# Two-layer graph kernel on one NeuronCore: half of the late node products from two-part operands, edge sums begun eleven tiles earlier, 29 gathers ahead of the stores

## What is computed

```python
edge_index = jnp.stack([src, dst])
x = _layernorm(x + gnn0(x, edge_index, node_vec, ...))     # all nodes
x = _layernorm(x + gnn1(x, edge_index, edge_weight, ...))  # edges, then per destination

# gnn0
neighbor_sum = segment_sum(x[col], row)                    # gather by edge, sum by node
mean_neighbor = neighbor_sum / max(deg, 1)
h_mean = (x + mean_neighbor) * 0.5 @ W_mean + b_mean
h_concat = concat([x @ W_ego + b_ego, mean_neighbor @ W_nb + b_nb])
gate = sigmoid(gate_weight * node_vec + gate_bias)
out = (1 - gate) * h_mean + gate * h_concat
```

## Time and profile before

| | |
|---|---|
| median of 3 runs | 2863.28 us |
| the profiled execution | 2864.34 us |
| its span, first to last instruction | 2862.5 us |
| busy in the span: PE, DVE, ACT, POOL | 92%, 84%, 65%, 55% |
| TensorE's granted clock, mean | 0.973 |
| float32 node products, line 961 | 1564 matmuls, 495 ns each as modelled |
| DMA traffic | 653.5 MB |

### The profile page before, as it was taken

How to read it: one execution, slowest core, us unless ns; L and a number is a source line. 1 busy time by engine, 2 the same in 40 slices (tenths; PEclk the granted TensorE clock), 3 DMA queues, 4 the chain that set the end, 5 groups by cost and what they waited for, 6 DMA issues and landing times. The chain is left out here.

```text
span 2862.5 us, 53163 instructions
## 1 busy us (share of the span) xinstructions
PE 2641.2 (92%) x14009; PEld 1610.8 (56%) x14009; DVE 2393.4 (84%) x7769; ACT 1851.0 (65%) x3839; POOL 1582.5 (55%) x1491
## 2 busy tenths in 40 slices
PE   4699989999999499999999999999999999976774
PEld 2466668788887255555555555555555555543442
DVE  8888877777777688888888888888888888878996
ACT  2355555666665277777777777777777777757885
POOL 0476727777776555454545454545455555306776
PEclk9799999999999699999999999999999999989998
DMA  9899986666665587777777777777777777647894
GB/s 346 298 350 350 351 295 202 198 199 203 203 204 183 155 211 220 213 220 214 220 213 222 214 222 212 219 218 221 213 223 213 222 212 217 180 131 239 276 281 149
DMA packets 544668, 653.52 MB, mean 228 GB/s; under 512 B 244334, under 2 KB 451882, under 8 KB 544550
## 3 DMA queue, kind: packets, MB, share of 16 engines
q1 hardware_dynamic: 468518, 440.38, 52.2%
q0 software_dynamic: 69472, 208.99, 23.4%
q10 hardware_dynamic: 6560, 2.84, 0.4%
HBM read 315.65 MB, written 299.10 MB: 215 GB/s over the span
## 5 line engine op out<-in xcount | busy, mean ns | idle before, releaser
L1242 ACT ACTIVATE hidT<-bank,b1c 128x512 f32<-128x512 f32 x490 | 336.7, 687 | 414.3 <-PE bank L1532 340.4
L1151 POOL TENSOR_TENSOR u_hc<-u_hc 128x1536 f32<-128x1536 f32 x98 | 270.1, 2756 | 550.9 <-issue 429.4
L961 PE MATMUL bank<-w_node,xT 128*128 128x384 f32 x1564 | 558.6, 495 | 15.1 <-ACT bank L584 15.0
L1532 PE MATMUL bank<-xh,w1h 128*128 128x512 f16 x1568 | 469.2, 381 | 23.3 <-DMA xh<-eh 15.7
L1532 PE MATMUL bank<-xl,w1h 128*128 128x512 f16 x1568 | 468.2, 380 | 0.0
L1532 PE MATMUL bank<-xh,w1l 128*128 128x512 f16 x1568 | 468.2, 380 | 0.0
L584 ACT ACTIVATE bank<-bias_all 128x512 f32<-128x512 f32 x391 | 234.3, 599 | 235.7 <-DVE H L689 234.3
L961 PEld LDWEIGHTS bank<-w_node,xT 128*128 128x128 f32 x1564 | 288.5, 193 | 161.4 <-ACT bank L584 17.2
L1548 PE MATMUL bank<-hidT,w2f 128*64 128x256 f32 x3136 | 360.1, 382 | 0.8 <-ACT hidT L1242 0.8
L1373 DVE STREAM_TRANSPOSE feat<-catT 32x256 f32<-32x256 f32 x784 | 342.5, 437 | 17.0 <-ACT catT L1251 2.4
L1354 DVE TENSOR_SCALAR hidT<-bank,b1c 128x512 f32<-128x512 f32 x294 | 220.6, 750 | 120.7 <-PE bank L1532 112.3
(11 more groups left out here) (255 smaller groups left out, 5199.3 us busy)
## 6 DMA issues: line engine op xcount, KB each, us to landing
hc_tab<-H SPq DMA_DIRECT2D x78, 680.0 KB
er<-edge_tab SPq DMA_DIRECT2D x98, 512.0 KB, 4.4
X<-in_x SPq DMA_DIRECT2D x78, 640.0 KB, 5.2
h_row<-hc_tab SPq DMA_DIRECT2D x97, 512.0 KB
out_x<-o_row SPq DMA_DIRECT2D x97, 512.0 KB, 5.0
edge_tab<-u_x SPq DMA_DIRECT2D x98, 256.0 KB, 3.9
edge_tab<-feat SPq DMA_DIRECT2D x98, 256.0 KB
hc_tab<-zero_row SPq DMA_DIRECT2D x18, 1344.0 KB
```

The source lines that it names most:

```text
L961: ins = t_.matmul(p[:, 0:384], xT[t // 2 % XR][:, t % 2, c * P:(c + 1) * P], w_node[:, c, :], start=False, stop=c == 1, skip_group_check=True)
L1151: g.tensor_tensor(c, c, u_hc[s][:, :, MULT:MULT + 3].unsqueeze(3).to_broadcast([P, 4, 3, P]), ALU.mult).then_inc(u_scaled, 1)
L1242: a.activation(hidT[m][:, :], bank[2 + m % 2][:, :], ACT.Relu, bias=b1c[:, m:m + 1])\
L1532: ins = t_.matmul(bank[2 + m % 2][:, :], w[:, c, m * P:(m + 1) * P], xx[s][:, :, :].rearrange("p (k c) e -> p c k e", c=2)[:, c, :, :], st ...
```

## The change

It edits the node block and one piece of the setup:

- From pair `SPLIT` = 92 on, every other pair of node tiles (92, 94, ... 194: 52 pairs, 104 tiles) has its product made from split operands: ACT's copy goes to `xhigh` (short type F32R), DVE makes `xlow` = bank 0 minus `xhigh` (`low_x`), and PE makes six matmuls a tile (high by high weight, high by low weight, low by high weight, for two halves) instead of two float32 products.
- `low_x(p)` stands in DVE's `side` of step 2p-3, one step behind ACT's copy of that pair. The `turn` of pair p+1, on PE's step 2p-2, now waits for it, since it reads bank 0.
- The setup makes `w_nodeh` and `w_nodel` on DVE.
- `xT` has 3 buffers instead of 4.
- `PUT_LAG` 13 becomes 29; `DECODE` 16 becomes 20; `SUMS` 195 becomes 184 and `SPAN` 177 becomes 188, so that the edge sums begin eleven tiles earlier and end at the same tile.

```diff
+        w_nodeh, w_nodel = sb("w_nodeh", [P, 2, 384], F32R), sb("w_nodel", [P, 2, 384], F32R)
...
                 st.done(v.tensor_copy(w_nbh[:, :, :], w_nb[:, :, :]))
-                st.wait()
+                st.done(v.tensor_copy(w_nodeh[:, :, :], w_node[:, :, :]))
+                st.wait()
+                st.done(v.tensor_tensor(w_nodel[:, :, :], w_node[:, :, :], w_nodeh[:, :, :].bitcast(F32),
+                                        ALU.subtract))
...
-        XR = 4
+        XR = 3
...
+        XS = 2
+        xlow = [tmp(f"xlow{b}", [P, 2, D], F32R) for b in range(XS)]
+        xhigh = [tmp(f"xhigh{b}", [P, 2, D], F32R) for b in range(XS)]
...
-        PUT_LAG = 13
+        PUT_LAG = 29
-        SORT, PHASES, DECODE, SUMS, SPAN, FIX = 0, 7, 16, 195, 177, 377
+        SORT, PHASES, DECODE, SUMS, SPAN, FIX = 0, 7, 20, 184, 188, 377
+        SPLIT = SUMS // 2 // 2 * 2
+        SPLITS = tuple(range(SPLIT, NT // 2 + 1, 2))
...
+                    to = xhigh[nth(p) % XS] if in_parts(p) else xT[p % XR]
...
+                def low_x(p):
+                    many = min(2, NT + 1 - 2 * p)
+                    dve.wait_ge(xt_copied, p + 1)
+                    if nth(p) >= XS:
+                        dve.wait_ge(p_ready, 2 * SPLITS[nth(p) - XS] + 2)
+                    q = nth(p) % XS
+                    v.tensor_tensor(xlow[q][:, 0:many, :],
+                                    bank[0][:, 0:many * D].rearrange("p (t d) -> p t d", t=many),
+                                    xhigh[q][:, 0:many, :].bitcast(F32), ALU.subtract).then_inc(x_low, 1)
...
+                    if now % 2 == 1 and in_parts((now - 1 + LEAD_X) // 2):
+                        low_x((now - 1 + LEAD_X) // 2)
...
                 def turn(p):
-                    if p:
+                    if in_parts(p - 1):
+                        pe.wait_ge(x_low, nth(p - 1) + 1)
+                    elif p:
                         pe.wait_ge(xt_copied, p)
...
+                    if in_parts(pair):
+                        pe.wait_ge(x_low, nth(pair) + 1)
...
+                            for part_, w in ((high, w_nodeh), (high, w_nodel), (low, w_nodeh)):
+                                n += 1
+                                ins = t_.matmul(p[:, 0:384], part_[:, c * P:(c + 1) * P], w[:, c, :], start=False,
+                                                stop=n == 6, skip_group_check=True)
```

More of the change, by code:

```diff
@@ L383, in build @@
         H = [tmp(f"H{r}", [P, HALF, HU]) for r in range(HR)]
-        XR = 4
+        XR = 3
         xT = [tmp(f"xT{b}", [P, 2, D]) for b in range(XR)]
+        XS = 2
+        xlow = [tmp(f"xlow{b}", [P, 2, D], F32R) for b in range(XS)]
+        xhigh = [tmp(f"xhigh{b}", [P, 2, D], F32R) for b in range(XS)]
+        x_low = sem("x_low")
         stats = tmp("stats", [P, TEN, 6])
@@ L444, in build, with nth, in_parts @@
         LASTR = (ET - 1) % AC
-        PUT_LAG = 13
-        SORT, PHASES, DECODE, SUMS, SPAN, FIX = 0, 7, 16, 195, 177, 377
+        PUT_LAG = 29
+        SORT, PHASES, DECODE, SUMS, SPAN, FIX = 0, 7, 20, 184, 188, 377
+        SPLIT = SUMS // 2 // 2 * 2
+        SPLITS = tuple(range(SPLIT, NT // 2 + 1, 2))
+        def nth(p):
+            return (p - SPLIT) // 2
+        def in_parts(p):
+            return p in SPLITS
         PRODS = (5, 6, 7)
@@ L575, in copy_x @@
                     many = min(2, NT + 1 - 2 * p)
-                    a.activation(xT[p % XR][:, 0:many, :], bank[0][:, 0:many * D].rearrange("p (t d) -> p t d", t=many),
+                    to = xhigh[nth(p) % XS] if in_parts(p) else xT[p % XR]
+                    a.activation(to[:, 0:many, :], bank[0][:, 0:many * D].rearrange("p (t d) -> p t d", t=many),
                                  ACT.Copy).then_inc(xt_copied, 1)
@@ L958, in product @@
                     p = bank[NODE[t % 3]]
-                    pe.wait_ge(xt_copied, t // 2 + 1)
+                    pair = t // 2
+                    if in_parts(pair):
+                        pe.wait_ge(x_low, nth(pair) + 1)
+                        high, low = xhigh[nth(pair) % XS][:, t % 2, :], xlow[nth(pair) % XS][:, t % 2, :]
+                        n = 0
+                        for c in range(2):
+                            for part_, w in ((high, w_nodeh), (high, w_nodel), (low, w_nodeh)):
+                                n += 1
+                                ins = t_.matmul(p[:, 0:384], part_[:, c * P:(c + 1) * P], w[:, c, :], start=False,
+                                                stop=n == 6, skip_group_check=True)
+                        ins.then_inc(p_ready, 1)
+                        return
+                    pe.wait_ge(xt_copied, pair + 1)
                     for c in range(2):
```

## The result

The changed kernel takes 3024.67 us (median of 3 runs, 3018.76 to 3028.46) against 2863.28: a ratio of 1.0557, 95% interval 1.0542 to 1.0572. That is 161 us slower, where 8.9 slower (2872.2) was forecast, and far outside the range of 2843 to 2880. The profiled execution spans 3022.9 us against 2862.5.

What follows compares the result with a forecast made beforehand. PE was taken as the bound from 444 to 924 us. Setup +1.4, keys and sums -0.5, split +8.0 gave +8.9 on 2864.34: 2873.2 us profiled, 2872.2 us median; range 2843 to 2880, for 8 in 10.

Steps and rivals of the forecast that it cites:

- Rest: `xT` with three buffers, the end of the sums and all later blocks: no effect, 0 us.
- Setup, +1.4: Setup block: two more DVE operations on 128x768 for the weight parts add 1.4 us, between 0 and 1.5.
- Keys: Node block, read of the keys: four tiles, 6.0 us, move into DVE's 7.28 us wait; node tiles gain 6.0.
- Start of the sums: Node block, tile 184: first sum waits for its gather until 373.8; DVE stands 6.7 us, eating the gain.
- Last fill and the new wait: Node block: first scatter at 435.0 after the last zero fill; PE stands 8.8 us at step 207, until 441.2.
- the term -0.5: Node block, later keys and earlier sums together: the wait of 8.34 changes its cause and stays; -0.5 us.
- Split, +8.0: Node block, 46 pairs from 104 on: 25 waits for `xlow` cost 28.2 us, savings 20.2, net +8.0.
- The three bare places: Earlier trace, `turn` with only one product before it: DVE's low part would come late, waits 0.95, 1.16, 1.48 us.
- The clock rule: Node block: frequent waits of about 1 us among PE's matmuls could make the clock swing; taken as 0.
- the fourth rival: Node block: the clock swings, each of 25 bare waits costing 2.8 us: +70, 2942 us; chance 0.03.
- Rivals 1 to 3: Node block: bank 0 free in time, 2844.0 us, 0.20; fills in before scatters, 2860.6, 0.14; scatters become the bound, 2879, 0.10.

Runs made afterwards that it cites:

- the run with eight fills: The changed kernel with eight one-column fills on DVE ahead of its edge loop: 2878.40 us, ratio 1.0051 to the kernel before.
- the longer loop: The kernel before, DVE's edge loop head 104 instructions into a 256-instruction block, 24 more instructions (semaphore steps) a round: 2949.85 us in one run.
- slot 104: The kernel before with DVE's edge loop head placed 104 instructions into a 256-instruction block, so the body crosses its end: 2864.74 us in one run.
- the announced jump: The changed kernel with `hint_back_edge=True` on DVE's edge loop instead of a placed head; the text gives no time.

## Why the prediction was wrong, step by step

- **The step that failed** is "*Rest*": "The end of the sums and all later blocks keep their place, 0." Their order on the engines did stay, and their place in the work too; what did not was the place of DVE's loop in its own instruction stream. The change adds 104 instructions ahead of it, and that cost 147 us. That the shift ended at a dear slot is chance: with eight instructions more, the same change is 146 us faster. No rival had it: all of them stand in the block that the change edits. What could be seen beforehand: a loop on DVE behind the edit, 104 instructions, an `instruction` queue in the list. What could not: the slot that the loop has on the chip, and that a shift would be dear.
- **The node block** came out at 13.6 us by PE's first edge row (11.8 in the run with eight fills), 8.9 were forecast: right in sign and kind.
- *Setup, +1.4.* DVE's last part of the weights ends at 29.29 against 28.06: +1.2.
- *Keys.* The wait of 7.28 is down to 0.86 (1.3 forecast), and the read stands at 108.33:

```profile
108.33 0.26 DVE L780 TENSOR_SCALAR ids_at<-raw 128x196 int32<-128x196 int32 x1 [0.86 <-DMA edge_raw<-srt_tab]
```

- *Start of the sums.* DVE's wait for the first gather is there, 7.84 in place of 6.7, and the first sum runs at 375.75, not 373.8 (before: the earlier trace rows):

```profile
375.75 1.08 DVE L901 SCALAR_TENSOR_TENSOR acc<-acc,same,xg 128x256 f32<-128x256 f32 x2 [7.84 <-DMA xg<-in_x,pay]
```

PE stood 9.82 behind it, until 379.22:

```profile
379.22 1.11 PE L984 MATMUL bank<-ident,X 128*128 128x128 f32 x4 [9.82 <-DVE xlow L872]
```

The prediction used the wait to eat the gain, and left out what comes after: the granted clock of 366 to 389 us is 0.78, where before it was 1.00.
- *Last fill and the new wait.* The fill went out at 429.25 (425.5 forecast), the first scatter at 438.94 (435.0), and PE's new wait is there, 9.99 (8.8):

```profile
438.94 1.04 POOL L559 DMA_INDIRECT hc_tab<-cn,idx_s  x1 [31.02 <-DMA hc_tab<-zero_row]
```

```profile
446.12 0.66 PE L1042 MATMUL bank<-w_nbh,accT 128*128 128x384 f32 x1 [9.99 <-ACT cn L631]
```

Two stands of about 10 us in place of one of 8.34, and the second ends at 446.12 where 441.2 was reckoned: the term -0.5 measured +3.8 without the split. Of these 4.9 us too late, 3.9 were there at the first scatter, in the sum up to the last fill. Inside the node block this is the term that was mis-sized.
- *Split, +8.0.* Waits on the `turn` line for `xlow`, 444 to 924 us (25, 28.2 us forecast):

```profile
PE bank L984 <- DVE xlow L872: 19.0, 22, 1.9
```

That is 0.86 a wait where 0.95 to 1.48 was taken. With the setup it was to cost 9.4, and alone it measured 8.8 by PE's rows and 12.0 by the runs (7.4 to 16.9). The three bare places in the earlier trace rows foretold the waits in kind, but that the sum was met is partly luck. In the run with eight fills PE waits 18.7 us for `xlow`, and the edge block begins 8.0 later than without the split, 1.2 of them the setup; so the pairs saved an estimated 18.7 - 6.8 = 12 us where 20.2 were reckoned. Waits and savings were both taken too large, by 8 to 10 us, and the errors cancelled.
- *The clock rule.* The granted clock of 444 to 924 us is 0.99, but what is missing lies right behind the stand that ends at 446.12: from 444 to 460 us it is 0.80, and from 460 to 924 us, where all 22 waits are (the first ends at 471.2), it is 1.00. So this term was 0, and the fourth rival did not occur here. The section on psum-queue depth-cycling of the Trainium skill's page "TensorE: Matmul & The Clock Gate", weighed in the prediction, is not borne out by these 22 waits, and no run has them come more often. In the edge block the clock did fall, behind the stand of 4.65.
- Rivals 1 to 3 fell as well: bank 0 was not free in time, the fills were not in before the scatters, and POOL did not become the bound.

## What to carry to other kernels

An edit ahead of a rolled loop moves the loop in its engine's instruction stream, and a body of some 260 instructions can then cost several us at every jump back, far from the edit. So before blaming the edit, look at unchanged loops for idle time put down to "issue" once a round, and at the packets of the `instruction` queues; then shift the loop by a few instructions, or place its head, and time again. And an operation that another engine waits for belongs in the step in which its input arrives: moved one step, it made the changed kernel 21 us faster and the split alone 10, and only the first of the two then beat the kernel before.

## What the runs showed of the hardware

- A jump back on DVE that refetches takes five packets of 8.2 KB and makes it stand 6.2 us in the changed kernel (on average 3.9 and 2.3, ahead of the first and of the second operation of the loop), and once, some 4 us, in the longer loop.
- Whether it does is a matter of a few slots: eight instructions more ahead of the loop, 146 us less. Crossing one end of a block of 256 cost nothing at slot 104 (2864.74 us), and 24 instructions more in the body brought the five packets back (2949.85).
- Left open: the size and number of the pieces (four of 128 fits all runs but the announced jump, and is an estimate), why the longer loop stands once only, and why the announced jump fetched nothing.
